# A selective scan over 64 states: more drives made by TensorE and ScalarE, more read-outs on GpSimd, a transpose one chunk earlier

## What is computed

```python
# 256 channels are cut into 4 chunks of 64; each is widened to 128 inner channels; 16 states for each
dt = softplus(dt_proj(dbc[..., :4]) + dt_bias); Bs, Cs = dbc[..., 4:20], dbc[..., 20:36]
A  = -exp(A_log)                                        # (128, 16)
def step(h, (dt_t, B_t, C_t, x_t)):
    dA = exp(dt_t[:, :, None] * A)                      # decay
    h  = dA * h + (dt_t * x_t)[:, :, None] * B_t[:, None, :]   # drive
    return h, einsum('bds,bs->bd', h, C_t)              # read-out
y = ys + xc * D_param;  y = y * silu(z);  y = out_proj(y)
```

## Time and profile before

| | us |
|---|---|
| median of 3 runs | 1844.05 (1843.04 to 1844.74) |
| the profiled execution | 1846.15, of which the span of the core is 1844.4 |
| the four stretches of scans, from the first scan to the last read-out | 197.2, 195.4, 197.5, 197.1 |
| the experts and their routing, from about 1180 us on | some 660 |

### The profile page before, as it was taken

The page is one execution under the profiler, slowest core; times in us unless marked ns, Lnnn a source line. Parts: engine busy times, 40 slices in busy tenths (PEclk is TensorE's granted clock), DMA queues, the critical chain, the costliest instruction groups (busy, mean ns, idle before and its releaser), DMA issues. The chain is left out here.

```text
span 1844.4 us, 22487 instructions
## 1 busy us (share of the span) xinstructions
PE 1562.0 (85%) x6433; PEld 996.5 (54%) x6434; DVE 1182.3 (64%) x1368; ACT 946.9 (51%) x1758; POOL 1074.2 (58%) x574
## 2 busy tenths in 40 slices
PE   5588898988789888888898888773499999999997
PEld 2233335643335553333564333453388888888896
DVE  3399998489998579999658989846622222222222
ACT  6857665876664876775677666431022222222222
POOL 0499991279994159999037999400345555545543
PEclk9899999999999999999998999996699999999999
DMA  3256560156662057564025656552022222222221
GB/s 103 95 204 211 208 214 1 49 190 234 221 214 73 1 168 250 189 213 159 2 74 192 234 194 228 207 215 71 21 34 38 34 38 36 40 34 37 37 31 28
DMA packets 78400, 222.41 MB, mean 121 GB/s; under 512 B 12588, under 2 KB 31349, under 8 KB 74966
## 3 DMA queue, kind: packets, MB, share of 16 engines
q1 hardware_dynamic: 62390, 202.54, 31.6%
q0 software_dynamic: 15904, 18.66, 6.3%
HBM read 199.76 MB, written 19.82 MB: 119 GB/s over the span
## 5 line engine op out<-in xcount | busy, mean ns | idle before, releaser
L462 PE MATMUL psum<-HC_sb,ident_sb 128*128 128x512 f32 x768 | 371.4, 609 | 39.0 <-DVE HC_sb L1561 24.8
L462 PE MATMUL psum<-experts_sb 64*128 64x512 f32 (+5 forms) x882 | 275.3, 548 | 78.6 <-DVE HC_sb L1561 24.3
L1968 ACT ACTIVATE hgt_sb<-psum_moe,b_sb 128x256 f32<-128x256 f32 (+1 forms) x312 | 116.2, 455 | 380.8 <-PE psum_moe L1875 380.8
L1127 ACT ACTIVATE psum<-experts_sb 128x1024 f32<-128x1024 f32 x192 | 212.7, 1111 | 168.3 <-DVE experts_sb L1551 106.9
L1551 DVE TENSOR_TENSOR_SCAN experts_sb<-psum,DBX_sb 128x1024 f32<-128x1024 f32 x108 | 244.2, 2276 | 23.6 <-ACT psum L1127 17.2
L2120 DVE TENSOR_TENSOR YS_sb<-psum_moe,b_sb 128x256 f32<-128x256 f32 x71 | 30.2, 425 | 356.2 <-PE psum_moe L1875 356.2
L1875 PE MATMUL psum_moe<-XGT_sb,w1s_sb 128*128 128x256 f32 (+1 forms) x1248 | 254.1, 362 | 0.0
L1875 PE MATMUL psum_moe<-experts_sb,hgt_sb 128*128 x1136 | 251.7, 379 | 0.7 <-DVE YS_sb L2120 0.7
L1852 POOL DMA_INDIRECT out<-YS_sb,scat_sb x71 | 129.1, 1818 | 207.2 <-DVE YS_sb L2124 192.1
L462 PEld LDWEIGHTS psum<-HC_sb,ident_sb 128*128 128x128 f32 x768 | 139.4, 192 | 199.8 <-issue 101.7
L1875 PEld LDWEIGHTS psum_moe<-XGT_sb,w1s_sb 128*128 128x128 f32 x1248 | 219.0, 191 | 25.3
(11 more groups left out here) (298 smaller groups left out, 2379.4 us busy)
## 6 DMA issues: line engine op xcount, KB each, us to landing
DA_sb<-bc_rows SPq DMA_DIRECT2D x96, 512.0 KB, 4.8
X_XT_sb<-bc_rows SPq DMA_DIRECT2D x92, 512.0 KB, 4.1
experts_sb<-bc_rows SPq DMA_DIRECT2D x48, 512.0 KB, 5.1
SQ_sb<-bc_rows SPq DMA_DIRECT2D x48, 512.0 KB, 5.4
T_sb<-bc_rows SPq DMA_DIRECT2D x20, 512.0 KB, 5.8
experts_sb<-w1T SPq DMA_DIRECT2D x8, 1024.0 KB, 18.5
experts_sb<-w2T SPq DMA_DIRECT2D x8, 1024.0 KB, 20.4
X_sb<-x_tok SPq DMA_DIRECT2D x5, 1024.0 KB, 6.9
```

Source lines behind the costliest of these rows:

```text
L462: return nc.tensor.matmul(o, lhsT, rhs, start=start, stop=stop, **k)
L1127: nc.scalar.activation(DECAY_SB if is_turned(i) else decays[i % 2], DT[:, c, :], ACT.Exp, scale=a_neg[:, s:s + 1]).then_inc(da_ready, 1)
L1968: m = nc.scalar.activation(HGT[:, k, 4 * h + q, 0:w], psum[:, 2 * h + q // 2, (q % 2) * 2 * P:(q % 2) * 2 * P + w], ACT.Gelu, bias=b1[:, b ...
```

## The change

In chunk 0 nothing of the two lists moves. In the chunks 1 to 3, six states of sixteen are turned instead of four (1, 4, 6, 9, 12, 14 instead of 6, 9, 12, 15), and the read-outs on GpSimd go from 7, 8 and 8 to 10, 9 and 10 (with chunk 0, from 28 to 34 of 64). So in each sample GpSimd makes six drives fewer and six read-outs more, VectorE makes six read-outs fewer, and ScalarE and TensorE make six turned drives more. The scaled blocks of a turned state are spread over the two or three states ahead of it by a rule (`scaled_behind`) in place of the table. B's columns are kept for all 16 states, in the space of the FFN weights. The transpose of dt·x for the chunks 1 to 3 moves from state 2 of the chunk to state 12 of the chunk ahead. The load of the residual input moves from i = 18 to i = 36, and the four bias additions from 22, 25, 28, 31 to 41, 43, 46, 49.

```diff
-POOL_READS = ((2, 8, 10, 12, 14), (2, 4, 6, 8, 10, 12, 14), (0, 2, 4, 6, 8, 10, 12, 14), (0, 2, 4, 6, 8, 10, 12, 14))
-TURNED_DRIVES = (6, 9, 12, 15)
+POOL_READS = ((2, 8, 10, 12, 14), (0, 2, 3, 4, 6, 8, 9, 10, 12, 14), (0, 2, 3, 4, 6, 8, 10, 12, 14),
+              (0, 2, 3, 4, 6, 8, 9, 10, 12, 14))
+TURNED_DRIVES = ((6, 9, 12, 15),) + ((1, 4, 6, 9, 12, 14),) * (NC - 1)
...
+def scaled_behind(i):
+    gap = min(i - max((j for j in range(i) if is_turned(j)), default=i - 2), 2 if i % NS == 1 else 3)
+    return dict(zip(range(i - gap, i), ((4, 4), (2, 3, 3))[gap - 2]))
...
         def scaled_tile(c):
-            return (XC[:, 1, :] if c else log_tile(2)).rearrange("p (n d) -> p n d", n=NB)
+            return (XC[:, 1, :] if c >= 2 else log_tile(2)).rearrange("p (n d) -> p n d", n=NB)
...
-                    if s == TOK_AT + 1:
-                        pe.wait_ge(tok_copied, b * (NC + 1) + (c + 2))
+                    if on_pool(i - 1) and i - 1 in TOK_AT:
+                        pe.wait_ge(tok_copied, b * (NC + 1) + (TOK_AT.index(i - 1) + 2))
...
                     act.wait_ge(tok_turned, b * (NC + 1) + (c + 2))
+                    if c:
+                        act.wait_ge(scaled, b * turned_drives(NI) + turned_drives(c * NS))
...
-TOKENS_AT, NEXT_AT, X_AT, TOK_AT = 12, 15, 18, 2
-RESIDUAL_AT = (22, 25, 28, 31)
+TOKENS_AT, NEXT_AT, X_AT, LAST_DT_AT = 12, 15, 36, 9
+
+TOK_AT = (2, NS - 4, 2 * NS - 4, 3 * NS - 4)
+RESIDUAL_AT = (41, 43, 46, 49)
```

More of the change, by code:

```diff
@@ L90 @@
 MORE_AT = NS + 2
+LAST_IN_X = max(j for j in range(2 * NS) if is_turned(j))
 PRODUCT_IN = rotation(NI, 2, MORE_AT)
@@ L93, with drives_in_slot @@
 DRIVE_IN = rotation(pool_drives(NI), 3, pool_drives(MORE_AT))
+def drives_in_slot(k):
+    return sum(d % B_SLOTS == k for d in range(pool_drives(NI)))
 def rows_in_slot(k):
@@ L771, in dtx_turn @@
                 def dtx_turn(c):
-                    i = c * NS + TOK_AT
+                    i = TOK_AT[c]
                     assert on_pool(i) and not on_pool(i + 1)
@@ L827, in scans @@
                         turned_drive(i + 2)
-                    if i % NS == TOK_AT:
-                        dtx_turn(c)
+                    if i in TOK_AT:
+                        dtx_turn(TOK_AT.index(i))
                     c_row(i)
@@ L913, in bc_tokens @@
                 act.wait_ge(tok_turned, b * (NC + 1) + 1)
-                first, step = TURNED_DRIVES[0], TURNED_DRIVES[1] - TURNED_DRIVES[0]
-                at = psum[:, 4:6, :].rearrange("p g (n c k) -> p (g n) c k", n=4, c=NC)[:, :, :, first:NS:step]
+                at = psum[:, 4:6, :].rearrange("p g (n c k) -> p (g n) c k", n=4, c=NC)[:, :, :, 0:NS]
                 nc.scalar.activation(B_TOK, at, ACT.Copy).then_inc(tok_copied, 1)
@@ L1136, in scale_blocks @@
[L1136 to L1147, removed]
+                    j = next((j for j in range(i + 1, NI) if is_turned(j)), None)
@@ new lines, in scale_blocks @@
+                    if j is None or i not in scaled_behind(j):
+                        return
+                    behind, c = scaled_behind(j), j // NS
+                    done = sum(n for at, n in behind.items() if at < i)
+                    if done == 0:
+                        act.wait_ge(turned_ready, b * turned_drives(NI) + turned_drives(j))
+                        if j == turned_states[0]:
+                            act.wait_ge(dt_done, b * NC + 3)
+                    for n in range(done, done + behind[i]):
+                        m = nc.scalar.activation(scaled_tile(c)[:, n, :], DTX_TOK[:, n, :], ACT.Copy,
+                                                 scale=B_TOK[:, n, c, j % NS:j % NS + 1])
@@ L1149, in scans @@
+                    if done + behind[i] == NB:
+                        m.then_inc(scaled, 1)
+                turned_states = [j for j in range(NI) if is_turned(j)]
                 for i in range(NI):
                     decay(i)
[L1151 to L1155, removed]
+                    if i - 2 == TOK_AT[0]:
+                        dtx_tokens(0)
@@ L1156, in scans @@
                     scale_blocks(i)
+                    if i - 2 in TOK_AT[1:]:
+                        dtx_tokens(TOK_AT.index(i - 2))
                     if 4 <= i < 8 and after:
```

15 lines of the change are left out of this document (7 added, 8 removed).

## The result

The changed kernel took **1834.34 us** (median of 4 runs, 1832.81 to 1834.96), against 1844.1 before: a ratio of 0.9949, 95% interval 0.9936 to 0.9963. The forecast was 1836, with the forecast of a faster kernel at 65%. The profiled execution has a span of 1830.9 us against 1844.4.

What follows compares the result with a forecast made beforehand. GpSimd's fixed work and its idle time, about 7 us a sample, were taken as the bound; 4 x (2.1 - 0.1) = 8 us off the 1844.05 median gave 1836, forecast range 1830 to 1840 (53%), 8 in 10 within 1824 to 1850.

Steps and rivals of the forecast that it cites:

- The bound: Chunks 1 to 3: GpSimd's work stays (141.5 before, 141.4 after), so only its idle time can be won; 2.1 us a sample.
- GpSimd's idle time: GpSimd's waits in a sample, summed over chunk starts, shift and end: 7.0 us before, 5.1 after.
- Start of chunk 1: Scan 18 starts 1.1 us earlier, read-out 18 waits 1.9, read-outs 19 and 20 about 0.2 each; GpSimd's idle 3.2 becomes 2.3.
- Start of chunk 2: Read-outs 34 and 35 on GpSimd both wait for a scan, 0.5 + 1.4 us; idle 0.4 becomes 1.9, the order's cost.
- The shift: GpSimd's shift after state 38 waits 1.9 us for VectorE's small reciprocal; VectorE comes earlier, so 0.9 was taken.
- The end: Read-out 62 on GpSimd waited 1.5 us for its scan; with GpSimd running late the wait becomes 0.
- ScalarE's cover: ScalarE's 16 more blocks a chunk, 4.8 us, cost nothing; scan 22 about 1 us late, but GpSimd later still.
- The third rival: ScalarE and TensorE stretch the chain, decays 1 us late in each of two chunks: 1842 to 1846; 20%.
- The short distances: Five times a sample only 4.45 us remain for a row of C to land, median 4.0; 0.1 us a sample taken.
- The second rival: Late rows of C make it slower at the five short distances; landings with mean 5.5 us give 1857; 13%.
- The load of the residual input: Issued right behind the row of C for state 34, it holds read-out 34 up to 1.6 us, inside read-out 35's wait.
- more comes through: Chunk-start knots loosen too, GpSimd's idle goes to 3 instead of 5.1 us: 1828; ceiling, VectorE's whole 26.6 us, 1817.5; 12%.

Runs made afterwards that it cites:

- e5: The changed kernel with all four bias additions of a sample moved behind its last read-out on GpSimd: 1820.9 us, ratio 0.9872.
- e12: The kernel before the change, with only the bias additions moved behind the last read-out and GpSimd's small shift one state later: 1824.8 us, ratio 0.989.
- e9: e7 with the exponential's table loaded back on ScalarE right behind the square root at state 34: 1811.1 us, ratio 0.9815.
- e7: e5 with GpSimd's small shift one state later (40 instead of 39): 1821.1 us, ratio 0.9863.

## Why the forecast held, step by step

- **The bound.** "GpSimd's fixed work and its idle time" gave 2.1 us a sample; scan 16 to scan 63 gave 1.9, and four samples 8 us where 8 were forecast. The other 1.8 us of the median and 5.5 of the profiled span, forecast at 1836.4 and measured at 1830.9, have no row in these chunks; that they were small in the median is luck. That VectorE's relief of 6.7 us would not come through was right: its waits for drives grew from 3.8 to 6.2.
- **By chunk** the forecast was 47.2, 49.8 and near or over 48.5; measured were 47.2, 50.2 and 49.9.
- **GpSimd's idle time** was to go from 7.0 to 5.1 and went from 7.4 to 5.0. The places differ more than the sum, so part of the agreement is two errors that met. These are its waits at the starts of the chunks 1 and 2:

```profile
724.06 2.35 POOL L1257 TENSOR_TENSOR HC_sb<-X_XT_sb,experts_sb 128x1024 f32<-128x1024 f32 x1 [0.51 <-PE psum L474]
729.54 2.37 POOL L1257 TENSOR_TENSOR experts_sb<-X_XT_sb,experts_sb 128x1024 f32<-128x1024 f32 x1 [0.82 <-DVE experts_sb L1567]
...
776.84 2.36 POOL L1257 TENSOR_TENSOR HC_sb<-X_XT_sb,experts_sb 128x1024 f32<-128x1024 f32 x1 [0.72 <-DVE experts_sb L1567]
782.90 2.37 POOL L1257 TENSOR_TENSOR HC_sb<-X_XT_sb,experts_sb 128x1024 f32<-128x1024 f32 x1 [1.40 <-DVE experts_sb L1567]
```

- **Start of chunk 1.** Idle was to go from 3.2 to 2.3. It is 0.51 + 0.82 = 1.3 in the changed kernel, and 0.33 more stands ahead of it: read-out 14 waits 0.80 for TensorE (before 0.47), read-out 16 waits 0.51. The transpose of dt·x and the turned drive of state 17 now stand ahead of those sums in TensorE's order; that they are the cause is read from the order. I had allowed up to 0.5 and hidden it in the wait of read-out 18, and that is where it went: 1.9 became 0.8.
- **Start of chunk 2.** 0.5 + 1.4 forecast, 0.72 + 1.40 measured. The shift: 0.9 forecast, 0.84 measured. The end: 0, and so it was.
- **ScalarE's cover.** Scans 21 and 22 wait 0.41 and 0.35 for decays, where I carried 1 us at scan 22. Later in the same chunk VectorE waited 0.21 and 0.95 for drives, so they may well have been covered, as said; no kernel shows it by itself. The third rival, new waits for decays over 4 us, did not come: 2.2 and 0.4 in all three chunks.
- **The short distances.** 0.1 us a sample was taken; no wait for a row of C is in the trace. The second rival falls by its own condition. The estimate of 3.2 us for a landing, from the fit in the Trainium skill, "DMA: Bandwidth & Descriptors", section "Anatomy of one DMA", stays under all of the landings here, 3.4 and more. The page gives that fit for transfers issued by GpSimd in software, and SyncE issues these, so it was not a measure for them.
- **The load of the residual input** near row 34 cost nothing that a row shows; the longest landing in the chunks 1 to 3 was 7.8.

What the forecast had too narrow is the sentence that GpSimd's idle time is all that can be won "while its own work stays as it is". It was true, and it drew the eye to idle time. The additions were in my sums as 5 us of fixed work in each sample, and I asked what they cost after the move and not why they stood among the scans at all. e5 and e12 show that these 5 us and one wait for a tiny instruction were the larger part of what VectorE lost: its waits in the chunks 1 to 3 went from 6.2 us before to 2.4 in e12.

The ceiling of the rival "more comes through", 1817.5, counts VectorE's relief alone. The change by itself stayed far above it; e9, with the same lists and three further moves, lies at 1811, under it, since those moves take away waits that were never in that sum.

## What to carry to other kernels

When two engines are both nearly full and feed each other, look at the short instructions that stand between their long ones, at what each waits for, and at whether another place in the stream would hold them, before moving long ones across. To tell which of two full engines is the bound, add a little work to one at a place where it waits and take a little off the other; in this case the busy shares did not tell. Test a rebalanced list again after each such repair, since here two lists, 6.7 us of VectorE's work apart, came out within 1 us a sample.

## What the runs showed of the hardware

- A load of an activation table took 1.28 us, and its place in ScalarE's stream, behind or ahead of the wait of the next decay, moved scan 35 by nearly all of it: chunk 2 took 47.2 us with it behind and 46.0 ahead (e7, e9).
- Products on GpSimd kept their length: their mean was 2.37 us before, and 2.37 to 2.38 in the changed kernel, with 29 read-outs among them in the chunks 1 to 3 instead of 23.
- Rows of C, 512 KB each, landed in 4.0 us in the median in both kernels, though 28 were asked for in the chunks 1 to 3 instead of 22.
